# A decoder layer's attention steps: masks first, cross scores in four row tiles, shared score banks

## The reference

```python
q, k, v = (einsum('ntc,hdc->nhtd', x, w) for w in (w_q, w_k, w_v))   # 16 heads of 64
a = softmax(where(causal_forbidden, -inf, einsum('nhtd,nhsd->nhts', q, k) / 8))
x1 = layernorm(x + (einsum('nhts,nhsd->nthd', a, v).reshape(...) @ w_o))
# cross attention on ctx: 16 heads of 16, mask (128 keys, the last up to 32 invalid)
x2 = layernorm(x1 + (softmax(where(mask == 0, NEG, qh @ kh.T / 4)) @ vh) @ Wo.T + bo)
# two groups of 32 experts, hidden 128, top 2 of each by router, SwiGLU, weighted; mean of the groups
out = layernorm(x2 + moe(x2))
```

## Time and profile before

| | |
|---|---|
| median of 3 runs | 5197.35 us (5183.77 to 5199.1) |
| the profiled execution | 5205.27 us, its span 5203.4 |
| TensorE busy | 4658.9 us, 90% |
| VectorE, ScalarE, GpSimd busy | 3827.1 (74%), 3274.2 (63%), 2779.5 (53%) |
| first stage, steady part | some 37 to 4075 us |
| second stage's first expert matmul | 4188.6 us |

### The profile page before, as it was taken

How to read it: one execution, slowest core, us unless ns; L and a number is a source line. 1 busy time by engine, 2 the same in 40 slices (tenths; PEclk the granted TensorE clock), 3 DMA queues, 4 the chain that set the end, 5 groups by cost and what they waited for, 6 DMA issues and landing times. The chain is left out here.

```text
span 5203.4 us, 129007 instructions
## 1 busy us (share of the span) xinstructions
PE 4658.9 (90%) x37824; PEld 3986.0 (77%) x37824; DVE 3827.1 (74%) x18185; ACT 3274.2 (63%) x12613; POOL 2779.5 (53%) x3874
## 2 busy tenths in 40 slices
PE   8988888888888888888888888888888789999998
PEld 7777777777777777777777777777777567877876
DVE  4777777777777777777777777777777736665888
ACT  6766666666666666666666666666666534444444
POOL 3455555555555555555555555555555545556777
PEclk9999999999999999999999999999999889999999
DMA  4111111111111111111111111111111459997998
GB/s 154 50 54 54 55 55 54 59 55 54 54 54 54 55 55 54 54 54 56 55 54 54 54 54 55 59 57 54 54 54 50 141 178 343 333 305 251 310 306 288
DMA packets 477418, 552.04 MB, mean 106 GB/s; under 512 B 55632, under 2 KB 408144, under 8 KB 476240
## 3 DMA queue, kind: packets, MB, share of 16 engines
q1 hardware_dynamic: 350800, 296.21, 17.9%
q0 software_dynamic: 52224, 146.87, 7.6%
q10 hardware_dynamic: 73728, 100.70, 6.4%
HBM read 266.21 MB, written 277.35 MB: 104 GB/s over the span
## 5 line engine op out<-in xcount | busy, mean ns | idle before, releaser
L875 ACT ACTIVATE prob<-prob,negmax 128x128 f32<-128x128 f32 x2048 | 796.8, 393 | 701.2 <-DVE negmax L991 701.2
L875 ACT ACTIVATE xprob<-xprob,xnegmax 128x128 f32<-128x128 f32 x2048 | 800.5, 402 | 10.1 <-DVE xnegmax L991 10.1
L1324 POOL DMA_INDIRECT y_d<-y,to x576 | 565.0, 981 | 366.0 <-DVE y L1466 287.7
L569 POOL CAST yTh<-yT 128x512 fp32r<-128x512 f32 x256 | 171.9, 671 | 1022.2 <-ACT yT L911 1022.2
L624 POOL DMA_INDIRECT xs_d<-xrow,place x512 | 541.2, 1057 | 133.6 <-issue 133.6
L991 DVE CUSTOM_DVE_ANT_0 prob<-bank,causal 128x128 f32<-128x128 f32 x2048 | 451.2, 283 | 204.2 <-PE bank L750 204.2
L1377 PE MATMUL bank<-moe,xgT 128*128 x2304 | 597.6, 382 | 1.0 <-issue 0.6
L588 POOL TENSOR_TENSOR rs<-spread_v,minus_half 128x1 f32<-128x1 f32 x256 | 145.4, 568 | 681.1 <-DVE spread_v L1064 681.0
L1027 DVE TENSOR_TENSOR prob<-prob,inv 128x512 f32<-128x512 f32 x512 | 461.7, 902 | 17.6
L1036 DVE RECIPROCAL xinv<-xtotal 128x4 f32<-128x4 f32 x512 | 87.7, 171 | 520.7 <-ACT xprob L875 520.7
L777 PE MATMUL bank<-ident,prob 128*128 128x128 f32 x2048 | 311.2, 275 | 172.6 <-DVE negmax L991 172.5
(11 more groups left out here) (173 smaller groups left out, 14570.0 us busy)
## 6 DMA issues: line engine op xcount, KB each, us to landing
xg<-xs_d SPq DMA_DIRECT2D x576, 129.0 KB
xs_d<-blank SPq DMA_DIRECT2D x248, 272.0 KB, 2.8
rows<-y_d ACTq DMA_DIRECT2D x256, 256.0 KB
xT_s<-xT SPq DMA_DIRECT2D x128, 128.0 KB
cT<-cT SPq DMA_DIRECT2D x128, 128.0 KB, 2.1
x_s<-x SPq DMA_DIRECT2D x128, 128.0 KB, 2.1
x_d<-x SPq DMA_DIRECT2D x128, 128.0 KB, 1.9
sums<-x_d ACTq DMA_DIRECT2D x128, 128.0 KB
```

What stands on the lines that cost most here:

```text
L569: nc.gpsimd.tensor_copy(yT_p[0][:, c, :], yT[:, :, :]).then_inc(y_high, 1)
L875: last = nc.scalar.activation(dst[:, h, :], dst[:, h, :], ACT.Exp, bias=src_bias[:, h:h + 1], scale=-1.0, accum_out=acc[:, h:h + 1])
L1324: nc.gpsimd.indirect_dma_start(y_d[:, :], bass.IndirectOffsetOnAxis(ap=to[:, m % NTO:m % NTO + 1].bitcast(U32), axis=0), y_s[q][:, :], Non ...
```

## The change

Orders. On TensorE the self transposes move behind three jobs, and o1 and o2 ahead of them; rank moves from the even step to the odd one. On VectorE the masks come first in each step; the previous step's last cross normalisation stands behind them, x1t's copy goes ahead of the second normalisation, weigh behind x2, place_tokens and rank_moves to the odd step's end. ScalarE takes the previous step's last cross exponentials at the head of a step, and the owners' copy from VectorE. On GpSimd the scatters move one step later and open_blocks, root and scatter change places.

Cross scores. Four matmuls of 256 columns on four quarters of the array's rows (32 each) in place of two of 512 on halves; a quarter holds two heads, so xkD holds two heads' keys per row in place of four.

Banks. Self and cross scores share banks 0 to 3, two heads of each in a bank, so VectorE waits for both kinds of scores before it masks the self ones, and the transposes wait for masks of both kinds (masked_out).

The diff, cut to its core:

```diff
-EVEN = ("qk0", "o2", "qk1", "x1t", "v1", "xq", "xv", "rank", "xy")
-ODD = ("qk2", "x2t", "qk3", "o1", "route", "xk", "v0", "xy")
+EVEN = ("qk0", "o2", "qk1", "x1t", "v1", "xq", "xv", "xy")
+ODD = ("qk2", "x2t", "o1", "route", "qk3", "xk", "rank", "v0", "xy")
 QK = ("qk0", "qk1", "qk2", "qk3")
-AFTER = dict(qk0=-4, qk1=-4, qk2=-3, qk3=-3, v0=-1, v1=0, o1=3, xk=3, x1t=4, xq=4, xv=4, o2=8, x2t=9, route=9, rank=10)
+AFTER = dict(qk0=-4, qk1=-4, qk2=-3, qk3=-3, v0=-1, v1=0, o1=3, xk=3, x1t=4, xq=4, xv=4, o2=8, x2t=9, route=9, rank=11)
...
-xkD = sb("xkD", [P, 2, KC, XHALF, P])
...
-hot = sb("hot", [P, NGRP, TOPK, E])
+hot = [sb(f"hot{p}", [P, NGRP, TOPK, E]) for p in (0, 1)]
...
+    sb(n, [P, NGRP, E]) for n in ("blocks", "first", "beyond", "rank_first", "new_first"))
+step_first, rows_of = new_first, beyond
...
+SCORES, PV, JB = banks[0:4], banks[4], banks[5:8]
...
+def self_score(h):
+    side, pair = divmod(h, PH)
+    return SCORES[pair // 2 * 2 + side][:, pair % 2 * P:(pair % 2 + 1) * P]
+def cross_score_of(h):
+    return SCORES[h // 2][:, (2 + h % 2) * P:(3 + h % 2) * P]
...
-    if n % 2:
-        return prob[:, :, :, :].rearrange("p s h k -> p (s h k)")
-    return xkD[:, :, :, :, :].rearrange("p b m h k -> p (b m h k)")
+    return (prob if n % 2 else xprob)[:, :, :, :].rearrange("p s h k -> p (s h k)")
...
-            for m in range(KC):
-                last = nc.gpsimd.tensor_tensor(keys[:, m, 1:XHALF, :], spread(keys[:, m, 0, :], 1, XHALF - 1),
-                                               spread(own_head[:, 1:XHALF], 2, P), ALU.mult)
-            last.then_inc(xk_others, 1)
+            nc.gpsimd.tensor_tensor(keys[:, :, 1, :], keys[:, :, 0, :], spread(own_head[:, 1:2], 2, P).broadcast_to([P, KC, P]),
+                                    ALU.mult).then_inc(xk_others, 1)
...
             if 0 in slots:
                 pool.wait_ge(xrow_ready, b + 1)
                 pool.wait_ge(place_ready, b + 1)
+                pool.wait_ge(owner_in, b + 1)
...
-            b = due(n, 11, NB)
+            b = due(n, 14, NB)
+            if b is not None:
+                scatter(b, (2, 3))
+            b = due(n, 12, NB)
             if b is not None:
                 open_blocks(b)
-            b = due(n, 12, NB)
-            if b is not None:
-                scatter(b, (0, 1))
             if split_pair(n) is not None:
                 x_low(split_pair(n))
             b = due(n, 8, NB)
             if b is not None:
                 root(1, b)
+            b = due(n, 3, NB)
+            if b is not None:
+                root(0, b)
             b = due(n, 13, NB)
             if b is not None:
-                scatter(b, (2, 3))
+                scatter(b, (0, 1))
...
-            b = due(n, 3, NB)
-            if b is not None:
-                root(0, b)
...
+        def banks_empty(n):
+            x = n - CROSS
+            if live(n - 2) and live(x - 2):
+                return
+            wait(pe, maxed, min(2 * n, ALL))
+            wait(pe, xmaxed, min(2 * x, ALL))
+            wait(pe, probT_in, min(2 * (n - 1), ALL))
+            wait(pe, xprobT_in, min(2 * (x - 1), ALL))
+        def masked_out(n, cross_side):
+            if not cross_side or not live(n - 1):
+                wait(pe, maxed, min(2 * n + 2, ALL))
+            wait(pe, xmaxed, min(2 * (n - CROSS) + cross_side + 1, ALL))
         def score(n):
             b, g = heads_of(n)
             if g == 0:
-                for name in QK:
-                    pe.wait_ge(moved[name], b + 2 - b % 2)
-            wait(pe, maxed, 2 * n)
-            wait(pe, probT_in, 2 * (n - 1))
+                pe.wait_ge(moved["qk3"], b + 2 - b % 2)
+            banks_empty(n)
...
-            wait(pe, xmaxed, 2 * x)
-            wait(pe, xprobT_in, 2 * (x - 1))
-            for side in (0, 1):
-                last = nc.tensor.matmul(CROSS_BANKS[side][:, :], xqT[b % 2][HALVES[side], c, :],
-                                        xkD[HALVES[side], b % 2, c, :, :].rearrange("p h k -> p (h k)"), start=True, stop=True)
+            banks_empty(x + CROSS)
+            for r in range(4):
+                rows = slice(r * ROWS, (r + 1) * ROWS)
+                last = nc.tensor.matmul(SCORES[r][:, 2 * P:4 * P], xqT[b % 2][rows, c, :],
+                                        xkD[rows, b % 2, c, :, :].rearrange("p h k -> p (h k)"), start=True, stop=True)
...
             pe.wait_ge(normed, 2 * (n - 1) + side + 1)
-            if live(n):
-                pe.wait_ge(maxed, 2 * n + side + 1)
-            else:
+            if side == 0:
+                masked_out(n, 0)
+            if not live(n):
...
             pe.wait_ge(xnormed, 2 * (x - 1) + side + 1)
-            if live(x):
-                pe.wait_ge(xmaxed, 2 * x + side + 1)
-            else:
+            if side == 0:
+                masked_out(n, 1)
+            if not live(x):
...
-                pe.wait_ge(moved["v0"], b + 1)
...
             if n % 2 == 0:
                 job(n, "qk0")
+                job(n, "o2")
+                job(n, "qk1")
                 turn(n, 0)
-                job(n, "o2")
                 turn(n, 1)
-                job(n, "qk1")
                 cross_turn(n, 0)
                 job(n, "x1t")
                 cross_turn(n, 1)
                 job(n, "v1")
                 job(n, "xq")
                 job(n, "xv")
-                job(n, "rank")
             else:
                 job(n, "qk2")
+                job(n, "x2t")
+                job(n, "o1")
                 turn(n, 0)
-                job(n, "x2t")
                 turn(n, 1)
+                job(n, "route")
                 job(n, "qk3")
                 cross_turn(n, 0)
-                job(n, "o1")
                 cross_turn(n, 1)
-                job(n, "route")
                 job(n, "xk")
+                job(n, "rank")
                 job(n, "v0")
             mix(n)
...
+        def owners(n):
+            b = due(n, 10, NB)
+            if b is None:
+                return
+            act.wait_ge(route_step, b * 6 + 6)
+            wait(act, placed[b % 2], b // 2 * PLACED)
+            nc.scalar.copy(xrow[b % 2][:, :, OWNER], choice[b % 2][:, :, :].rearrange("p g k -> p (g k)")).then_inc(owner_in, 1)
...
             move_y(n)
+            cross_exponentials(n - 1, 1)
             exponentials(n, 0)
-            move_turned(n, 0)
             move_qk(n, "qk2" if n % 2 else "qk0")
             exponentials(n, 1)
+            move_turned(n, 0)
             move_turned(n, 1)
-            move_qk(n, "qk3" if n % 2 else "qk1")
-            cross_exponentials(n, 0)
-            move_cross_turned(n, 0)
-            move_cross_turned(n, 1)
             if n % 2 == 0:
+                move_qk(n, "qk1")
+                cross_exponentials(n, 0)
+                move_cross_turned(n, 0)
+                move_cross_turned(n, 1)
                 move_v(n, "v1")
+                owners(n)
             else:
+                cross_exponentials(n, 0)
+                move_qk(n, "qk3")
+                move_cross_turned(n, 0)
+                move_cross_turned(n, 1)
+                soften(n)
                 move_xk(n)
                 move_v(n, "v0")
-            cross_exponentials(n, 1)
-            b = due(n, AFTER["route"], NB)
-            if b is not None:
-                act.wait_ge(moved["route"], b + 1)
-                nc.scalar.activation(soft[:, :], below[:, :], ACT.Exp).then_inc(soft_ready, 1)
...
             dve.wait_ge(scores, n + 1)
+            wait(dve, xscores, n - CROSS + 1)
             wait(dve, turned, 2 * (n - 1))
...
-            wait(dve, placed[p], b // 2 * PLACED)
-            nc.vector.tensor_copy(xrow[p][:, :, OWNER], choice[p][:, :, :].rearrange("p g k -> p (g k)"))
...
         def even_step(n):
-            place_tokens(n)
             masked(n)
             cross_masked(n)
+            cross_normalise(n - 1, 1)
             b2 = job_of(n, "o2")
             if b2 is not None:
                 steps2 = residual(n, "o2", 1, norm2_step, sum2, x1b[b2 % 2], x1b_ready, b2 + 1)
             normalise(n, 0)
             if b2 is not None:
                 variance(steps2, 1)
-            weigh(n)
+            move_transposed(n, "x1t")
             normalise(n, 1)
             if b2 is not None:
...
-            move_transposed(n, "x1t")
+            weigh(n)
             cross_normalise(n, 0)
...
-            cross_normalise(n, 1)
         def odd_step(n):
-            rank_moves(n)
             masked(n)
             cross_masked(n)
+            cross_normalise(n - 1, 1)
+            move_transposed(n, "x2t")
             normalise(n, 0)
-            move_transposed(n, "x2t")
             if split_pair(n) is not None:
                 wait(dve, made["v1"], 2 * split_pair(n) - 2)
                 x_split_high(split_pair(n))
             normalise(n, 1)
-            cross_normalise(n, 0)
             b1 = job_of(n, "o1")
             if b1 is not None:
```

(32 more changed lines are left out.)

36 lines of the change are left out of this document (19 added, 17 removed).

## The result

The changed kernel takes 4677.35 us in the median of 4 runs (4674.7 to 4678.94); the kernel before, on the same chip, 5193.44 (5183.77 to 5199.1). The ratio is 0.9007, 95% interval 0.8992 to 0.9023. The forecast was 4680. The profiled execution took 4678.94, its span 4677.2; TensorE is busy 4486.3 us, 96% of it (90% before).

The account below looks back on a forecast made before the run. TensorE, busy 90%, was taken as the bound, with two holes per even step. A pair of 27.58 - 0.72 + 0.70 = 27.56 us against 31.67 saves 526: 5205 - 526 + 5 = 4684, about 4680 against the median; range 4575 to 4855.

Parts of the forecast that it names:

- The holes: TensorE's two waits in even steps, before the first transposes (1.54 us) and before xq (2.27); both were to close.
- The second hole: TensorE's wait for x1T before xq in even steps, 2.27 us lost; forecast to close with margin 0.6.
- The slow clock spells: Stretches partly at 1.2 GHz after TensorE stood still, 0.28 us a pair; forecast to go with the holes.
- Cross scores in row tiles: Cross scores on TensorE: four matmuls on quarters take 0.60 us instead of 0.96, saving 0.72 a pair.
- What is late next: Stalls expected next on TensorE: for xqT before the odd step's cross scores, and before rank; mean 0.35 us each.
- GpSimd's key spreading: Spreading keys on GpSimd: two small products instead of two and a half large, about 0.9 us less, on no path.
- rival (a): The loop through VectorE from scores to xqT and the next cross scores holds: 4760 to 4850 us; chance 0.18.
- Rival (c): Slower: GpSimd's queue delays root(1) behind two indirect DMAs and open_blocks; 5340 us at 4.5 us per DMA; chance 0.03.
- Margin 1.0: Slack between self masks done (4.4 us into a step) and the self transposes (5.6), stated as 1.0 us.
- Owners' copy off VectorE: Moving the owners' copy to ScalarE: VectorE loses 1.25 us, ScalarE gains some 0.3 of its idle time.
- Tail: One more step before the last scatter, behind the last batch: +5 us, ends -5 and +15.
- Port locks: VectorE and GpSimd SBUF work counted as blocking each other through an exclusive shared port lock, held for the whole instruction.

Follow-up runs that it names:

- the split late: The changed kernel with VectorE's copy x_split_high moved behind top_two in odd steps; 4859.99 us, ratio 0.9323.
- the normalisation first: The changed kernel with the previous step's last cross normalisation ahead of the masks again on VectorE, in both steps; 4798.05 us, ratio 0.9225.

## Why the prediction was right, and where not

**The holes.** Right, and for the reason given. The turns came at 5.55 (forecast 5.6) and waited for nothing, xq at 8.99 (forecast 8.8). Undoing either move brings waits back: 1.3 a step, and 2.5 a pair. The second hole closed more narrowly than forecast: x1T's copy ends at 8.85, not 8.2, so its margin is 0.14 and not 0.6. Which part of VectorE's new order makes the masks early is shown for the cross normalisation alone; the places of place_tokens and rank_moves, and GpSimd's new order, were not undone by themselves.

**The slow clock spells.** They went, as forecast (granted clock 1.00), but 0.28 a pair was too small for them. I took it as 31.67 less 31.39, and 31.67 is pulled down by the filling steps. With the pipeline full the pair of before is 32.08, so 0.69 above the one seen closely; the even step around takes 18.53 (2069.65 to 2088.18) in place of 16.91. Whether the clock makes all of the 0.69 was not worked out.

**Cross scores in row tiles.** The mechanism was right and the size off, and this is the term that was mis-sized: 0.72 a pair forecast, 0.46 measured. The cross scores take 0.64, not 0.60, and the self scores 0.09 more, since each step now goes through a third tile shape; with halves they are at 0.99 again. I had put the change of shape down once, at the cross scores. The Trainium skill ("TensorEngine Tiling (Array Packing)", Key Properties) says that switching the mode drains TensorE, and the rows agree in kind: the self scores take 0.09 more once another shape follows them. From the 3.07 times of the Trainium skill ("TensorE: Matmul & The Clock Gate", Measured speedup vs the span model) the estimate was 0.63, and the row shows 0.64, in which what the changes of shape cost is included. A pair without any stall then is 27.07 (2026.69 to 2053.76, from the end of one odd step's cross scores to the next) where the forecast's terms gave 26.86.

**What is late next.** The two places were right, and so was the size: with the pipeline full a pair takes 27.81, 0.74 above the one without a stall, where the forecast had 0.70. (The waits of the list come to 0.56, since a bracket shows less than is lost: 0.57 against 0.84 at rank, above.) So the full pipeline's pair is 0.25 longer than the forecast's 27.56: 0.21 of work (0.26 by the tiles, 0.05 back elsewhere) and 0.04 of stalls. The saving of such a pair is 4.27 (32.08 less 27.81) against 4.11: 0.41 more by the pairs of before that were longer than the one seen closely, 0.25 less by tiles and stalls. That the mean over the whole stage, 27.58, meets 27.56 is luck: the filling steps, which the forecast left out, pull it down.

**GpSimd's key spreading, "about 0.9 less, and is on no path".** Wrong, and the largest error of reasoning: given back alone it costs 2.5 a pair. Had it not been shortened, the loop of rival (a) would have held, at more than (a)'s 4760 to 4850: the run takes 5032. My own text had xqT at 13.5 with no margin, and root(1), which xqT hangs on, in the queue that the spreading shortens; the path had the spreading in it. Rival (c), the same queue seen from the other side, needs root(1) to end at 13.9; it ends at 9.5 (2021.07 + 0.57, less 2012.14), in the forecast's 8.7 to 9.6.

**"Margin 1.0" at the turns.** I took 1.03 for o2, from the overlapping length of one record. From start to start it is 0.67 (2015.41 to 2016.08). The turns came at 5.55 all the same because the scores took 1.74 in place of 1.60 and the second projection 1.61 in place of 1.53: the terms' errors nearly cancel. The sum was also read wrongly: its 5.6 less 4.4 is a margin of 1.2, and without the second projection the turns would have waited 0.3 by it, not 1. Measured, the margin is 0.8 (5.55 less 4.76).

**Owners' copy off VectorE, 1.25.** Its length was not its work: behind weigh the same copy takes 0.16, and the 1.25 was the time until GpSimd's product was through (2008.68 to 2010.09). What taking it away brought in its old place no run shows.

**Tail and median.** The tail cost 10.4, forecast 5, bounds -5 and +15. The second stage gave 15.6 that I didn't forecast; without it the run would have been near 4693, so that the median came within 3 us of 4680 is luck. In all the profiled executions here the time behind the last self score lies between 1120 and 1161 us, with no code of it changed; I found no settled cause.

Port locks were counted as they turned out: the product that starts beside GpSimd's SBUF work takes 1.79 where GpSimd's takes 1.29 (2004.62 to 2005.91) and the product alone 0.69; the masks, whose scores come from PSUM, take 0.28 to 0.29 beside it as elsewhere. That agrees with the exclusive lock of the Trainium skill ("SBUF — State Buffer", the list under the diagram).

## What to carry to other kernels

Before calling a shortened or lengthened operation free, follow everything that is queued behind it on its in-order engine to the next engine's work: here 0.95 us on GpSimd was worth 2.5 us a pair, and a copy put later to close a stall of 0.57 cost more than it closed. Place work of a mover engine in the time it already spends waiting (0.9 before the odd masks), not behind something that others wait for. Read durations from start to start, and count a change of tile shape at each side of the new shape. Take a pair's length from the full pipeline, not from a mean that holds its filling, and check a wait's named releaser by whether the gap to it stays the same.

## What the runs showed that was not expected

A GpSimd operation of 0.95 us was amplified to 2.5 us a pair by three things in a row: a wait of 1.29, a collision that made a 0.69 product 1.59, and the slower clock behind the hole (0.97 and 0.95 granted over 500 to 3500 us, 1.00 in the changed kernel). TensorE's self scores take 1.09 instead of 1.00 when the next matmuls use another tile shape. And the profile's name for a wait can mislead. GpSimd's odd scatter, which stands ahead of root(1) in its queue, waits some 2.1 us each time (224.8 us in 107 times), by the profile for a DMA that clears rows:

```profile
2009.46 0.17 DVE L1136 TENSOR_SCALAR place<-rank_b 128x4 int32<-128x4 f32 x1
```
```profile
2010.39 1.09 POOL L634 DMA_INDIRECT xs_d<-xrow,place  x1 [2.09 <-DMA xs_d<-blank]
```

But it starts 0.76 us after VectorE's place has ended, and 0.76 to 0.78 after it in each of 48 odd steps of three runs (the changed kernel, the split late, the normalisation first). A DMA that has nothing to do with place wouldn't keep that distance, so place ends the wait: GpSimd's root, VectorE's x1 and place, and the scatter follow on each other in every odd step.
